# Releasing gathers by VectorE's blocks, and a last layer on standing halves with adjacency pieces widened by ScalarE

## What is computed

```
L0: out = relu(adj @ (h @ W0) + b0); result row i = max over j with adj[i,j] != 0 of out[j]      (pooling)
L1: [h, adj @ h] @ W1
L2: a hyperbolic layer: weighted sums adj @ (gamma*XW) and adj @ (gamma-1), then norms and tanh
L3: z = leaky(lap(adj, h) @ W31 + b31); S[i,:] = exp(-|z_i - z_j| / 2) kept at the 4 nearest j
    out = d * ((S + adj) @ (d * h)) @ W32 + b32,   d = 1 / sqrt(row sums of S + adj)
```

## Time and profile before

| | us |
|---|---|
| median of 3 runs (lowest, highest) | 1754.88 (1749.66, 1757.28) |
| the profiled execution, its own time | 1755.54 |
| its span, from the first to the last instruction | 1753.8 |
| busy: PE, DVE, ACT, POOL | 1538.2, 1257.8, 767.4, 631.2 |

### The profile page before, as it was taken

How to read it: one execution, slowest core, us unless ns; L and a number is a source line. 1 busy time by engine, 2 the same in 40 slices (tenths; PEclk the granted TensorE clock), 3 DMA queues, 4 the chain that set the end, 5 groups by cost and what they waited for, 6 DMA issues and landing times.

```text
span 1753.8 us, 31129 instructions
## 1 busy us (share of the span) xinstructions
PE 1538.2 (88%) x8740; PEld 920.7 (52%) x8740; DVE 1257.8 (72%) x3409; ACT 767.4 (44%) x1175; POOL 631.2 (36%) x822
## 2 busy tenths in 40 slices
PE   4999999865887888798969999999999999858997
PEld 3777777522333333576745666777444444424554
DVE  7799999964777777648856666632899999923434
ACT  3444444323555545358742223765565565500000
POOL 5333333356555556534510001333000000165664
PEclk8999999977999999899989999999999999978999
DMA  8688787523323223333303223443000000033442
GB/s 287 222 306 302 277 292 293 184 67 109 85 80 78 78 77 85 95 110 102 96 13 120 84 89 109 126 124 117 0 0 12 6 6 6 19 108 119 138 133 78
DMA packets 160459, 202.99 MB, mean 116 GB/s; under 512 B 11940, under 2 KB 133730, under 8 KB 152208
## 3 DMA queue, kind: packets, MB, share of 16 engines
q1 hardware_dynamic: 136000, 174.68, 30.0%
q0 software_dynamic: 11728, 21.33, 4.7%
q10 hardware_dynamic: 12672, 6.29, 1.2%
HBM read 178.85 MB, written 28.38 MB: 118 GB/s over the span
## 4 chain that ended last, share of the span: by engine, by line
PE 55%; DVE 17%; issue 16%; POOL 4%; DMA 3%; ACT 3%; DVEq 1%; POOLq 0%; ACTq 0%; SPq 0%
PE bank L707 19%; PE bank L773 9%; PE bank L585 8%; DVE partsA L2294 5%; PE bank L627 5%; PE bank L882 4%; POOL gath L1456 3%; PE bank L590 3%; PE bank L561 2%; DMA gath<-pool_features,idx_now 2%; PE bank L614 2%; DVE cand L1767 2%; PE bank L548 1%; DVE hn L1680 1%; PE bank L883 1%
## 5 line engine op out<-in xcount | busy, mean ns | idle before, releaser
L707 PE MATMUL bank<-partsB,panel 128*128 128x387 bf16 (+1 forms) x2048 | 368.2, 338 | 56.4 <-issue 34.3
L707 PEld LDWEIGHTS bank<-partsB,panel 128*128 128x128 fp8e4 x2048 | 204.5, 100 | 215.9 <-issue 74.8
L882 PE MATMUL bank<-wide,partsA 128*128 128x512 f32 x512 | 263.2, 596 | 6.3 <-ACT rows L1253 4.9
L1767 DVE MAX8 cand<-bank 128x8 f32<-128x128 f32 x1024 | 217.7, 292 | 10.4 <-PE bank L590 6.4
L984 ACT ACTIVATE first<-bank 128x512 fp8e4<-128x512 f32 x256 | 139.2, 596 | 196.1 <-PE bank L614 116.4
L627 PE MATMUL bank<-first,partsB 128*128 128x512 fp8e4 x768 | 202.7, 403 | 19.9 <-issue 17.3
L585 PE MATMUL bank<-partsA,panel 128*128 128x387 bf16 x1024 | 212.0, 329 | 6.4 <-DVE cand L1767 5.3
L1900 DVE TENSOR_TENSOR gath<-gath,bank 128x512 f32<-128x512 f32 x240 | 161.3, 683 | 76.6 <-remote 49.2
L1456 POOL DMA_INDIRECT gath<-pool_features,idx_now x160 | 171.1, 1069 | 109.3 <-DMA gath<-pool_features,idx_now 43.2
L773 PE MATMUL bank<-adj_ring,layer_halves 128*128 128x512 f32 x768 | 198.4, 409 | 8.8 <-POOL adj_ring L1520 5.4
L937 ACT ACTIVATE panel<-bank 128x1024 fp8e4<-128x1024 bf16 x128 | 131.1, 1025 | 146.4 <-PE bank L561 146.4
(11 more groups left out here) (281 smaller groups left out, 2147.1 us busy)
## 6 DMA issues: line engine op xcount, KB each, us to landing
rows<-in_adj SPq DMA_DIRECT2D x64, 1024.0 KB, 7.2
panel<-adjT_panels SPq DMA_DIRECT2D x192, 256.0 KB
panel<-adjT_panels SPq DMA_DIRECT2D x64, 512.0 KB
adjT_panels<-panel SPq DMA_DIRECT2D x32, 512.0 KB, 3.0
gath<-pool_features,idx_now POOLq DMA_INDIRECT x160
overflow_maxima<-wide POOLq DMA_DIRECT2D x1, 2048.0 KB, 21.0
tail_maxima<-wide POOLq DMA_DIRECT2D x1, 2048.0 KB, 25.7
pool_features<-gsc ACTq DMA_DIRECT2D x8, 256.0 KB, 2.3
```

Of the source, the lines that this page charges most:

```text
L707: i = pe.matmul(bank[q][:, 0:3 * w], panel[:, q, j, :], of_block if w < FE else parts_of[u][:, j, :], start=(j == 0), stop=(j == NT - 1))
L882: pe.matmul(o[:, :], zs[:, q % 2, :], zT[:, c * 512:(c + 1) * 512], start=True, stop=False)
L1767: i = dve.max(cand[:, ch * BPB + b, :], bank[4 + ch % 4][:, b * P:(b + 1) * P])
```

## The change

1. **Pool stage.** `rows_landed` and the wait for the landed longer rows go. GpSimd waits instead until VectorE has taken a given pair of blocks: tile 0 of a group after the last pair of the group before, tile 1 after pair 3 of its group, the longer lists after pair 6, tile 2 after pair 8, tile 3 after pair 11.
2. **Last stage.** The three bf16 parts are replaced by the two float32r halves, in buffers of their own (`last_high`, `last_low`) in the space of the parts; GpSimd makes the low half in one subtraction. The product is the wide one: 8 pieces per group, a ring of four slots in the space of `rows`, all 64 pieces widened by ScalarE, 8 products of 512 columns per piece, turned back on TensorE. VectorE's first addition reads the turned product from PSUM, so that the sum over three parts (L1703) goes. The output is stored by SP.
3. **Waits of the last gathers.** Tiles 0 and 2 of a group wait for TensorE's count of used ring slots (6 and 2 pieces of the product before theirs), tiles 1 and 3 for nothing new.

```diff
-ON_POOL = ((1, 2, 4, 7), (1, 4, 7))
-ON_ACT = ((0, 3, 5, 6), (0, 2, 3, 5, 6))
+ON_POOL = ((1, 2, 4, 7), (1, 4, 7), ())
+ON_ACT = ((0, 3, 5, 6), (0, 2, 3, 5, 6), (0, 1, 2, 3, 4, 5, 6, 7))
+TURN_OF_TILE = (None, 3, 8, 11)
+TURN_OF_LONGER = 6
...
+            def last_pieces(g, r):
+                for c in range(NG):
+                    wait_widened(sp, 2, g - 1, c)
+                    load_piece(g, c)
+                store_out(g - 3, r)
...
-            first_products(5, 2, None)
-            with pe.Fori(1, NG) as g:
-                for q in range(G):
-                    product(5, g, q, 2)
+            for g, c in FIRST_PAIR:
+                operand_of_pair(5, c)
+                wide_product(2, g, g, c)
+            def last_turn(g, r, first=False):
+                pe.wait_ge(s_wideT, g + 2 * NG - 1)
+                for c in range(NG):
+                    if first and c < 2:
+                        turn_back(2, c, c, True)
+                    if not first and c == 1:
+                        turn_back(2, g - 1, 1 - r)
+                    wide_product(2, g, r, c)
...
-            part1(5, NG - 2)
             similarities(NG - 1)
             second_std(NG - 1)
+            act.wait_ge(s_keyused, NT + 1)
+            widen(2, 0, 0)
             last_operand(NG - 1)
-            part1(5, NG - 1)
+            widen(2, 0, 1)
+            act.wait_ge(s_keyused, NT + 2)
+            for g, c in FIRST_PAIR[2:]:
+                widen(2, g, c)
+            widen(2, 2, 0)
+            take_wide(2, 0, 0, True)
+            widen(2, 2, 1)
+            take_wide(2, 1, 1, True)
+            def last_turn(g, r, second=False):
+                for c in range(2 if second else 0, NG):
+                    if c == 3 and not second:
+                        take_wide(2, g - 1, 1 - r)
+                    widen(2, g, c)
...
-            def rows_landed(g, q):
-                pool.wait_ge(s_gath[q], 16 * MAIN * (g + 1))
+            def pair_taken(g, pair):
+                pool.wait_ge(s_fp_used, HT * g + pair + 1 + 2)
...
-                if q in (1, 3):
-                    rows_landed(g, q - 1)
+                if q:
+                    pair_taken(g, TURN_OF_TILE[q])
+                elif not first:
+                    pair_taken(g - 1, HT - 1)
...
+                pair_taken(g, TURN_OF_LONGER)
...
-                pool.wait_ge(s_over_gath, 16 * MIDDLE * (g + 1))
...
             def last_gathers(g, r, q):
                 t = g * G + q
-                pool.wait_ge(s_sum, NT + t + 2)
+                if q % 2 == 0:
+                    pool.wait_ge(s_slot, 2 * NG * NG + g * NG + 2 * q - 2)
...
-                    take_product(5, (g + NG) * G + q, q)
-                    dve.wait_ge(s_sum, (g + NG) * G + q + 5)
...
-                                                 agg[:, q, 0:F], ALU.mult, ALU.add).then_inc(s_last, 1)
+                                                 agg[:, q, 0:F] if k else bank[2 + r][:, q * P:(q + 1) * P],
+                                                 ALU.mult, ALU.add).then_inc(s_last, 1)
```

More of the change, by code:

```diff
@@ L86, in program @@
             rows = shared.enter_context(nc.sbuf_tensor("rows", [P, 2, N], F32))
+        with ExitStack() as shared:
+            last_adj = shared.enter_context(nc.sbuf_tensor("last_adj_ring", [P, RING, G, G * P], F32R))
+        last_ring = [last_adj[:, k, :, :] for k in range(RING)]
         over_sel = rows[:, 0, 0:NT * P // 2].bitcast(BF16).rearrange("p (t s) -> p t s", t=NT)
@@ L380, in widen_waits, with ring_of, wide_slot, turned @@
             eng.sem_inc(waited[who], 1)
-        def wide_slot(g, c):
-            return ring[slot_of(g, c)[1] % RING].rearrange("p b (q i) -> p q b i", q=G)
+        def ring_of(w, g, c):
+            return (last_ring if w == 2 else ring)[slot_of(g, c)[1] % RING]
+        def wide_slot(w, g, c):
+            return ring_of(w, g, c).rearrange("p b (q i) -> p q b i", q=G)
+        def turned(w, r):
+            return (last_turned if w == 2 else wideT)[:, r, :]
         def wide_source(c):
@@ L506, in _, with turn, store_out @@
             other_pieces(0)
[L508 to L515, removed]
-                    for q in range(G):
[L517 to L523, removed]
+            def turn(g, peeled):
+                for q in range(G):
+                    if peeled:
+                        wait_widened(sp, 0, NG - 1, 2 * q)
+                        wait_widened(sp, 0, NG - 1, 2 * q + 1)
+                    else:
+                        sp.wait_ge(s_lprod, g * G + q - G + 1)
+                    load_panel(g, q)
+            turns(sp, turn)
+            for c in range(NG):
+                sp.wait_ge(s_lprod, (NG - 1) * G + c // 2 + 1)
+                load_piece(0, c)
+            other_pieces(1)
+            def store_out(g, r):
+                sp.wait_ge(s_fin, g + 1)
+                sp.dma_start(out[ds(g * G * P, G * P), :].rearrange("(t p) f -> p t f", p=P),
+                             fin[:, r, :, :]).then_inc(s_out[r], 16)
+            for c in range(NG):
+                wait_widened(sp, 1, NG - 1, c)
+                load_piece(0, c)
+            for g, c in FIRST_PAIR:
+                wait_widened(sp, 2, g, c)
+                load_piece(g + 1, c) if g == 0 else load_piece(2, c)
+            def last_pieces(g, r):
+                for c in range(NG):
+                    wait_widened(sp, 2, g - 1, c)
+                    load_piece(g, c)
+                store_out(g - 3, r)
+            last_pieces(3, 0)
+            with sp.Fori(2, NG // 2) as h:
+                last_pieces(2 * h, 1)
+                last_pieces(2 * h + 1, 0)
+            for g in range(NG - 3, NG):
+                store_out(g, g % 2)
+            for r in range(2):
+                sp.wait_ge(s_out[r], 16 * (NG // 2))
             sp.wait_ge(s_g2, 16 * NG)
@@ L1007, in take_wide @@
                 act.wait_ge(s_slot, (NG * (g + 1) if not first_pair else 2 * NG - 1 + g) + w * NG * NG)
-                act.copy(wideT[:, r, :], bank[r][:, :]).then_inc(s_wideT, 1)
+                act.copy(turned(w, r), bank[r][:, :]).then_inc(s_wideT, 1)
             def clear(g):
@@ L1258, in turn @@
                                 last_operand(g - 2)
-                        if q == 2 and not second_group:
-                            part1(5, g - 2)
                         if q == (2 if last else 3):
```

68 lines of the change are left out of this document (42 added, 26 removed).

## The result

| | before | changed |
|---|---|---|
| median of 4 runs, us (lowest, highest) | 1753.8 (1749.66, 1757.28) | 1788.82 (1773.46, 1800.33) |
| ratio to before, 95% interval | | 1.0184 (1.0149 to 1.0219) |
| profiled execution, its own time / its span | 1755.54 / 1753.8 | 1785.46 / 1783.7 |
| busy: PE, DVE, ACT, POOL | 1538.2, 1257.8, 767.4, 631.2 | 1499.4, 1235.0, 882.7, 623.9 |

The change was forecast to gain 60 us and lost about 32 (the ratio leaves out its execution of 1800.33 us, which was in the slower of two states). The place of the loss is read from VectorE's timeline of the changed kernel: first blocks of groups 2 and 7, the end of the stage, and the first maximum after it. They answer to the earlier trace rows.

The account below looks back on a forecast made before the run. GpSimd was taken to bound the pool stage, a quarter of its chain being landing waits, and its gather issue the changed last stage. Gains of 31 and 29 us sum to 60: 1755.5 − 60 = 1695.5, forecast 1695, range 1668 to 1724.

Parts of the forecast that it names:

- Step 1: Pool stage: without landing waits the period falls from 42.2 to 38.0 us (34 to 40); groups 2 to 7 gain 25.
- rival D: Pool stage: the stops at group heads vanish, period 34, 24 us more gained, 1671 us; chance 0.12.
- The group head: Pool stage: SP waits 14.6 us per group for stored maxima, pieces come late, VectorE has nothing for 4.70 us.
- Step 2: End of the pool stage: earlier rows remove VectorE's wait and TensorE's wait for casts; gain 6 us (3 to 9).
- the case for which the text gave 3.6: End of the pool stage: a late VectorE maximum among GpSimd's casts costs a cast; gain 3.6 us rather than 6.
- Step 3: Last stage: the new product takes 16.2 us per group, ends near 1677, and is no longer the bound.
- Step 4: Last stage: gathers issue back to back but for one stop, winning back product waits; gain 29 us (5 to 40).
- E: Last stage: slow issue of 0.65 us a product holds on; pool gain eaten at f = 0.5; about 1781 us; chance 0.04.
- B: Last stage: TensorE's slow issue comes before the first turned product, GpSimd's stop grows by about 21, 1716 us; chance 0.12.

Follow-up runs that it names:

- e1: The kernel before with only the pool-stage part of the change: 1654.27 us beside a before of 1699.09, ratio 0.9733.
- e7: The kernel before, unedited, run once more for its profile: 1699.54 us in one execution.
- e6: The changed kernel, unedited, timed once more: 1664.87 us beside a before of 1701.9, ratio 0.9783.
- e2: The changed kernel with the pool stage's old landing waits, so the last-stage part alone: 1712.36 us beside 1699.09, ratio 1.0078.
- e12: The changed kernel without the 160 gathers of tiles 0 to 3 in the pool stage: 1704.83 us beside a before of 1761.45, one execution.
- e11b: The changed kernel with GpSimd waiting for landed rows after each tile's 4 gathers in the last stage: 1811.06 us beside 1761.45, one execution.

## Why the prediction was wrong

- **Step 1, the period of the pool stage, failed.** Its account of GpSimd's chain was right: the landing waits were a quarter of it, and they went. The sentence that failed is "What is queued behind each wait on GpSimd is the next tile's gathers ...", with the bounds 34 to 40 built on it: it counted what the waits cost and did not ask what they gave or covered. The floor of 31 to 34 took VectorE's blocks at 0.97 us each, and had no term for the time that they stand behind TensorE. Its range for groups 2 to 7, a gain of 14 to 48 us, held no loss. Measured: 45.4 us where TensorE is held, 34.8 where it isn't (rival D's floor of 34). Without holds the part gains 45 us (e1), inside the range of 13 to 61.
- **The group head.** The earlier trace rows were read as SP's wait causing the stop. In e7, the same kernel, SP waits for the stored maxima up to 18.1 us in a group, and VectorE has no such stop. It was a hold, in the only run of 11 indirect DMAs.
- **Step 2, the stage's end: 6 us, measured 6.1** in the first comparison (from the last block to tile 30's index search 808.3 us before, 802.2 after). The maximum of 5.79 us is one of 0.41 there. In e6 against e7 it was 2.8 us (806.1 against 803.4): there VectorE's last maximum over the blocks took 6.74 us beside GpSimd's casts instead of 0.69. That is the case for which the text gave 3.6. By the Trainium skill's rule of the shared ports ("SBUF — State Buffer", section "SBUF: two separate sides") one of the two engines waits for the other's whole instruction. The 6.74 agrees with that, but not with the part that the first comer keeps the ports: VectorE's row begins at 665.84, GpSimd's three casts at 666.47, and VectorE ended after them.
- **Step 3, the product's pace: right where nothing is held.** ScalarE takes a product every 14.9 us in e2 (1580.00, 1594.88, 1609.77), against 16.2 forecast.
- **Step 4, the last gathers.** The first gather (1560.92 − 27.0 = 1533.9 in the time of before, forecast 1535.5) and the stop at tile 2 of group 1 (11.5 forecast, 12.38 in e6) were right. The term failed in its other half, "the other 43 are waiting for products": these waits were holds, and the change has holds as well: from its first to its last gather it takes 210 us (1560.92 to 1770.47), where the kernel before takes 203. Where there are none, part 2 can only lose its stop (e2: 13 us slower, where the forecast had a gain of 29, bounds 5 and 40).
- **The rival with the right sign was E**, at 0.04: TensorE's slow issue eats both gains, 1781 us forecast, 1788.8 measured. That the numbers are near is luck: E had the whole loss in the last stage, which lost 3 us, and kept the pool stage's gain of 31, where 33 were lost. It had the engine, not the place or the cause: it took the gap of the earlier trace rows as a trait of one stage's code, so its break-even at half of the products said nothing of the pool stage. B's reading by the Trainium skill's rule on instruction fetches ("Runtime: NRT & Kernel Launch", section "Instruction fetch mechanics") is not borne out: the fetches recorded took 0.3 to 1.8 us each, and e6 runs the same code without the gap.
- **Two sums.** The upper ends of the pool stage's terms add up to 48 + 8 + 0 + 9 = 65, not 61, and the chances of "faster" to 0.91, not 0.92. Neither bears on the miss.

What stays open: why TensorE is held at all, why on one chip and not on four others, and by what path. The runs show that it takes gathers, and that pauses after each 4 prevent it in the last stage. They don't show that the removed landing waits were such pauses for the pool stage. One rival is untested: in the traces with holds part of all engines' semaphore records is missing (VectorE has a record for 2128 of its 2307 updates in the changed kernel, and for all in e6), so the recording itself may take part, and no run here settles that.

## What to carry to other kernels

A wait that you remove has more sides than what it costs its engine: what its pause lets happen elsewhere, and which waits of other engines it covers. Before you price its removal, lay the idle times of all other engines beside the runs of the waiting one, and if simultaneous stops without a releaser lie in its busy runs, treat them as one effect, which a faster kernel will meet uncovered. And time a kernel of before on more than one chip: a 43 us wait that is in one chip's trace and not in another's is not there to be won.

## What the runs showed of the hardware

- TensorE's semaphore updates can arrive up to some 20 us after the end of the products that its rows show, in stretches where GpSimd issues indirect DMAs back to back, and only there: 8.2 us for the transposes above; ScalarE's longest such wait was 22.0 us. Between the two stages, from 752 to 1490 us of the changed kernel's trace, no recorded update of TensorE is later than the 1.1 to 1.6 us that L926 has in e6 too. ScalarE's recorded updates showed no such delay anywhere.
- The effect was there in the first comparison and on one chip of the later runs (before 1761 us), and absent on four chips (before 1697 to 1705 us). Between such chips the kernel before differs by 55 us and the changed one by about 124 (1788.8 against 1664.9).
- In the pool stage it vanishes without 20 of a group's 23 gathers (e12), and in the last stage with a pause of some 2.4 us after each 4 of them (e11b). Both are single executions on one chip.
- A VectorE maximum of 0.69 us took 6.74 us beside GpSimd's casts (e6).
